# Graph attention on one Trainium2 core: the inverse row sums are widened by GpSimd and turned by four transposes a pair, in place of eight products with the identity

## What is computed

```python
feat = einsum('nf,hfo->hno', x, W)
e = leaky_relu(attn_self[:, :, None] + attn_neigh[:, None, :], 0.2)
e = e + MASK_VAL * (1.0 - adj)          # adj is the layer norm of the other input
alpha = softmax(e, axis=-1)             # each row is divided by its sum
out = einsum('hnm,hmo->hno', alpha, feat) + b
return elu(out)                         # heads side by side
x = x + gat(gat(ctx))
```

## Time and profile before

| | us |
|---|---|
| median of 3 runs | 2304.65 (2304.18 to 2306.5) |
| profiled execution, its own time | 2300.46 |
| its span | 2298.7 |
| outside the span | 1.8 |
| graph attention stage, in the span | 0 to 616 |
| mean granted TensorE clock, in the span | 0.902 |

### The profile page before, as it was taken

How to read it: one execution, slowest core, us unless ns; L and a number is a source line. 1 busy time by engine, 2 the same in 40 slices (tenths; PEclk the granted TensorE clock), 3 DMA queues, 4 the chain that set the end, 5 groups by cost and what they waited for, 6 DMA issues and landing times. The chain is left out here.

```text
span 2298.7 us, 33608 instructions
## 1 busy us (share of the span) xinstructions
PE 1841.5 (80%) x8271; PEld 904.8 (39%) x8272; DVE 1461.6 (64%) x3126; ACT 1051.0 (46%) x1893; POOL 881.0 (38%) x949
## 2 busy tenths in 40 slices
PE   5588766887547999999982298888889429999994
PEld 2243333434344555555542022222222414444442
DVE  5777766777585565565555377777775575555552
ACT  5577766777333332233223156666667422222221
POOL 5465665666303555555542111111111013444441
PEclk8799987999778999999995589999999759999997
DMA  4100211110254789878556911111111626998884
GB/s 138 51 38 38 64 66 56 38 38 29 92 186 113 174 185 235 211 185 209 113 87 184 169 35 52 52 51 50 50 50 33 218 86 179 227 229 230 231 210 110
DMA packets 202160, 275.34 MB, mean 120 GB/s; under 512 B 83500, under 2 KB 121868, under 8 KB 200972
## 3 DMA queue, kind: packets, MB, share of 16 engines
q1 hardware_dynamic: 156955, 171.18, 24.4%
q0 software_dynamic: 38544, 97.02, 20.9%
q10 hardware_dynamic: 6561, 5.98, 1.4%
HBM read 204.44 MB, written 73.37 MB: 121 GB/s over the span
## 5 line engine op out<-in xcount | busy, mean ns | idle before, releaser
L1891 DVE TENSOR_REDUCE a_negmax<-a_m 128x1 f32<-128x512 f32 x512 | 328.1, 686 | 102.8 <-PE a_m L1747 101.2
L283 POOL TENSOR_TENSOR g_near<-g_mask,g_tb 128x512 f32<-128x512 f32 x256 | 322.5, 1275 | 155.6 <-DVE g_emin L544 153.6
L1839 ACT ACTIVATE a_prob<-a_s 128x1024 f32<-128x1024 f32 x256 | 260.6, 1021 | 142.6 <-PE a_s L1758 134.5
L365 PE MATMUL g_pt<-g_ident,g_p 128*128 128x128 f32 x1024 | 186.0, 314 | 130.3 <-DVE g_pT L553 121.2
L1283 PE MATMUL f_gu_bank<-f_wgu,f_xT 128*128 x768 | 267.9, 492 | 6.8 <-issue 3.6
L1747 PE MATMUL a_m<-a_kT,a_qT 112*128 (+1 forms) x512 | 198.3, 398 | 83.4 <-DVE a_negmax L1891 39.0
L474 ACT ACTIVATE g_p<-g_e,g_emin 128x512 f32<-128x512 f32 x256 | 183.3, 716 | 121.9 <-DVE g_emin L544 119.9
L1249 POOL DMA_INDIRECT tokens<-f_y,f_ids x96 | 151.1, 1573 | 220.2 <-DMA tokens<-f_y,f_ids 173.5
L1283 PE MATMUL s_gu_bank<-s_wgu,s_xT 128*128 128x512 f32 x512 | 232.5, 597 | 2.3 <-ACT s_xT L1335 1.6
L365 PEld LDWEIGHTS g_pt<-g_ident,g_p 128*128 128x128 f32 x1024 | 127.5, 157 | 257.9 <-DVE g_pT L553 205.2
L544 DVE CUSTOM_DVE_ANT_0 g_e<-g_near,g_h 128x512 f32<-128x512 f32 x256 | 173.3, 677 | 60.6 <-ACT g_h L459 31.7
(11 more groups left out here) (295 smaller groups left out, 2807.3 us busy)
## 6 DMA issues: line engine op xcount, KB each, us to landing
s_wgu<-in_L_ffn_w_gate_up SPq DMA_DIRECT2D x32, 1024.0 KB
f_wgu<-in_L_ffn_gate_up_proj SPq DMA_DIRECT2D x32, 768.0 KB
s_wd<-in_L_ffn_w_down SPq DMA_DIRECT2D x32, 512.0 KB, 4.1
a_qT<-q_parts SPq DMA_DIRECT2D x224, 64.0 KB, 2.2
g_tb<-neighbours SPq DMA_DIRECT2D x8, 1536.0 KB, 7.7
f_wd<-in_L_ffn_down_proj SPq DMA_DIRECT2D x32, 384.0 KB, 5.4
q_parts<-p_part SPq DMA_DIRECT2D x48, 128.0 KB, 2.3
g_tb<-neighbours SPq DMA_DIRECT2D x8, 512.0 KB, 4.3
```

The costliest lines, as they stand in the source:

```text
L283: pool.tensor_tensor(near[:, n % LAG, :], mask[slot][:, local % NT, :], t_all[k % SLOTS][:, local // NT, :], ALU.add).then_inc(near_ready, 1)
L365: last = nc.tensor.transpose(pt_bank[n % PT_BANKS][:, c, :], prob[:, n % LAG, c * P:(c + 1) * P], ident[:, :])
L1839: nc.scalar.activation(prob[n % QR][:, :, :], s_bank[n % RING][:, :, :], ACT.Exp).then_inc(p_ready, 1)
L1891: V.tensor_reduce(negmax[k % RING][:, st, head:head + 1], m_bank[n % RING][:, :], X_AXIS, ALU.max, negate=True).then_inc(m_read, 1)
```

## The change

`rinv` is first widened by GpSimd: a copy of 128x512 elements into a new buffer `rwide`, in which each inverse row sum stands 64 times (`spread_sums`, once a pair). TensorE then turns `rwide` in four transposes of 128x128 instead of the eight products of 64x128. GpSimd makes the copy at the end of its unit 6 of the pair's finishing block, behind `near` and, where there is one, behind `mask_tile`; TensorE reads it in step 3 instead of step 2. A semaphore, `rwide_ready`, goes with it.

```diff
+        rwide = sb("g_rw", [P, RING, NT, 2, F_OUT])
+        rwide_ready = sem("rwide_ready")
...
+                def spread_sums(pr):
+
+                    pool.wait_ge(rinv_ready, pr + 1)
+                    if pr >= RING:
+                        pool.wait_ge(r_ps, pr - RING + 1)
+                    pool.tensor_copy(rwide[:, pr % RING, :, :, :], bass.AP(rinv, pr % RING * PAIR, [[RING * PAIR, P], [1, NT], [NT, 2], [0, F_OUT]])).then_inc(rwide_ready, 1)
...
                         if 0 <= t < NT:
                             mask_tile(m, t)
+                    if n >= PAIR and n % PAIR == 6 and n // PAIR <= ALL_PAIRS:
+                        spread_sums(n // PAIR - 1)
...
-                    if step == 2:
-
-                        pe.wait_ge(rinv_ready, pr + 1)
+                    if step == 3:
+
+                        pe.wait_ge(rwide_ready, pr + 1)
...
-                        for u in range(PAIR):
-                            t, hh = divmod(u, 2)
-                            last = nc.tensor.matmul(r_bank[hh * F_OUT:(hh + 1) * F_OUT, t, :],
-                                                    bass.AP(rinv, pr % RING * PAIR + hh * NT + t, [[RING * PAIR, P], [0, F_OUT]]), ident[:, :],
-                                                    start=True, stop=True)
+                        for t in range(NT):
+                            last = nc.tensor.transpose(r_bank[:, t, :], rwide[:, pr % RING, t, :, :].rearrange("p h o -> p (h o)"), ident[:, :])
                         last.then_inc(r_ps, 1)
```

## The result

| | us |
|---|---|
| changed kernel, median of 4 runs | 2327.49 (2325.26 to 2328.6) |
| kernel before, median of 4 runs | 2305.57 (2304.18 to 2307.92) |
| ratio, 95% interval | 1.0086 (1.0072 to 1.0101) |
| profiled execution of the changed kernel, its span | 2328.6, 2326.8 |

The change makes the kernel 0.86% slower, about 20 us. The prediction was 2320, with 2308 to 2333 as its range.

What follows compares the result with a forecast made beforehand. The first 616 us were taken as a ring of four engines, paced block by block. Step and slack -1.1, mask blocks +13.5, clock +3 and tail +0.3 sum to +15.7 us: 2320 on the median, range 2308 to 2333.

Steps and rivals of the forecast that it cites:

- Mask blocks: Blocks 1, 13, 17: TensorE waits for GpSimd's copy behind the third mask tile; +13.5 us, ends 9.8 and 17.5.
- the bare chain: Blocks 1 and 17: copy, transposes, `g_rall`, exponential and branch delay VectorE's unit 7, without half-clock extra; +2.2 us each.
- GpSimd's copy: In ordinary blocks: 0.65 us a pair, 21 us in all, mostly in GpSimd's idle time, costing nothing there.
- TensorE's durations: Products 1.09 us a pair at full clock, 1.98 at half; transposes free 0.45 or 0.86, 20 us in all.
- The step from 2 to 3, full blocks: Blocks 6, 10, 22, 26 lose 0.25 us each; 5, 9, 21, 25 gain 0.5 and 4, 8, 20, 24 gain 0.45.
- The step from 2 to 3, the 17 other blocks: Blocks 7, 11, 23, 27 and the plain ones: -0.1 to +0.35 us each, taken as +0.1, together +1.7.
- The clock in the other blocks: Ten non-mask half-clock blocks: L397's first half 1.4 us longer if only products raise the clock; +3, ends 0 and 14.
- rival (1): First stage: full clock effect, 14 us instead of 3, mask blocks at 17.5; +31 us, 2335, halfway 2328; chance 0.18.
- Tail: Pair 31, finished with no work beside it: copy +0.65 us and a hand-over against 0.45 shorter transposes; +0.3.
- Signs: Changed profile: block 13 TensorE idle 8 to 10 us, `g_xo` 5 later; mask blocks +3.5 to +6.5, others under 1.

Runs made afterwards that it cites:

- the early copy: Changed kernel with GpSimd's copy in blocks 1, 13 and 17 made ahead of the first mask tile instead of behind the third; 2314.36 us, ratio 1.0039.
- the probe: Kernel before with 200 transposes, 100 products, 200 transposes of 128x128 back to back on TensorE in the copy-out stage, nothing reading them; no total time given.
- the two with extra products: Kernel before plus eight unread identity products in step 0: of every pair, 2299.48 us (0.9971); of all but the eight full blocks, 2294.35 us (0.9941).

## Why the prediction was right

The time lies in the range, and on the side that was forecast. For the mask blocks the mechanism was right; for the rest the number was near by luck. By its steps:

- **Mask blocks (+13.5 taken, ends 9.8 and 17.5).** Right: +12.4, and the early copy took the wait away. The upper end is 16.8 by its own terms (5.4 + 2 and twice 2.2 + 2.5). The first half of the products took 3.04 us in block 13 (3.32 forecast), 2.51 in block 17 and 1.94, the full-clock value, in block 1. Blocks 1 and 17 lost 2.3 each, the 2.2 of the bare chain and not the 3.5 taken; block 13 lost 7.8, more than its 6.5.
- **GpSimd's copy (0.65 us, hidden elsewhere).** Right: 0.62 us, and outside the mask blocks TensorE waited for it only in the tail.
- **TensorE's durations.** Right: 0.60 us a spread at the full clock, 1.06 to 1.12 at half. But 15 of the 32 spreads lay at half clock wholly or in part, not 13; with 15 the freed time is 21 us, and the upper end of the clock's term 17 instead of 14.
- **The step from 2 to 3, full blocks.** Half right. Blocks 5, 9, 21 and 25 gained 0.64 each (0.5 forecast), and 4, 8, 20 and 24 together 2.6 (1.8). Blocks 6, 10, 22 and 26, forecast at +0.25 each, changed by +0.1, -0.15, +0.1 and -0.2: nothing was lost there.
- **The step from 2 to 3, the 17 other blocks (+0.1 each, +1.7).** Wrong, and it is the same error as in the next term: I read the slack of these blocks at the clock that they had. The products moved alone cost 29 us.
- **The clock in the other blocks (+3 taken, ends 0 and 14).** Sized wrong, and by the wrong mechanism. The blocks outside the mask and full groups lost 19 us (9.5 in the five, 9.0 plain with the tail, 0.9 in blocks 2 and 3), of which the two terms and the tail together had 5.0. I had looked at the rise of the clock behind the products, and asked what kind of work raises it. The first half of the products was to take 1.4 us more; in blocks 28 to 30, where the forecast placed its sign, it took 2.2 us instead of 1.94. What came instead was a fall of the clock in five blocks in which it had not been low, over the spread and the transposes around it. That the kind of work decides, the ground of rival (1), fell with the probe.
- **Tail (+0.3).** The stretch before the scaling of pair 31 grew by 1.7 us, with 3 us of half clock; TensorE waited 2.0 us there for the copy.
- **Signs.** TensorE's idle time of 9.03 us in block 13 and ScalarE's 10.30 came as named; `g_xo` came 7.7 us later against the third mask tile, where 5 were forecast against unit 5. The blocks outside the mask ones were to grow by under 1 us: blocks 3, 7, 11, 14, 18, 19, 27, 28, 29 and 31 grew by 1.05 to 3.15.

The blocks sum to +25.7 in the profiled executions, of which the one of before lay 5 us below its median; the ratio of the runs gives +20. The forecast of +15.7 comes near since the mask blocks were right, the clock's term stood in the range with its upper end, and blocks 4 to 6, 8 to 10, 20 to 22 and 24 to 26 gave back 5.3 us, where 2.8 were forecast; and the ratio is 6 us below the sum of the blocks. The time measured is nearly the 2328 that stood as half of rival (1), whose mechanism was not the one at work.

What stays open: why the clock falls. With the spread in step 3 and no extra products it fell in the five blocks 25 times of 25, and with the products in step 2 never in 15 (before and the two with extra products); but most of the falls came ahead of the place that the step changes, behind the same rows of TensorE. With the transposes in step 2 it held in 19 and 27 and fell in 7, 11 and 23, although 11 and 27 are of one length (16.1 us) and one make. A kernel that only shifts the blocks in time was not run, nor was one kernel profiled several times; so that the time at which the blocks stand decides is a rival that no run excludes.

## What to carry to other kernels

A helper's instruction put on a queue is as early as that queue at its place, not as its inputs: where the queue elsewhere in the loop waits for a later unit than its reader is at, it makes the reader wait for that unit, so look at the rare blocks first. And where an engine's clock changes within the stage, slack has to be read at both clocks: a wait of 0.36 us that a block swallows at the full clock was 1.24 us at half, and was not swallowed. Moving one piece of work by one unit changed the clock in blocks where it had held, and this could not be read off the rows of these blocks; so compare the clock block by block after every such move. A little work in the gaps can be worth more than a saving, and has to be tried.

## What the runs showed of the hardware

Transposes of float32 without gaps bring TensorE from 1.2 to 2.4 GHz and hold it there: 0.50 to 1.00 within the first 4.3 us of the row, 1.00 for its other 19.7 us, and, behind 22.5 us of products, for the 22 us of the second row. And useless work paid: eight products of 64x128 in each of 24 pairs, 1.1 to 2.0 us each time, made the kernel before 0.6% faster (0.9941); half clock in its first stage fell from 133 to 89 us in the profiled executions.
